# Transformer layer on eight cores: the token buffer is cleared during attention, scatters go tile by tile, x gets five buffers and the first expert weight comes in four parts

## The reference, cut to what matters

```python
xn = _layernorm(x)
s  = _L0_attn_ref(xn, Wq, Wk, Wv, Wo, norm_w)
h  = xn + _mla(_rmsnorm(xn, g1), ...)            # h2 in the kernel
t  = _rmsnorm(h, g2)                             # rows that are routed
top_v, top_i = top_k(t @ gate_w, 2); gates = softmax(top_v)
out = h + sum over the 2 experts of gate * (silu(t @ w1[e]) @ w2[e])
return x + s * _silu(out)
```

## Time and profile before

| | us |
|---|---|
| median of 3 runs (range) | 1723.77 (1721.16 to 1821.45) |
| profiled execution, time | 1732.94 |
| profiled execution, span of its slowest core (core 6) | 1731.4 |
| spans of the 8 cores | 1681.5 to 1731.4 |
| TensorE busy | 1386.5 (80%) |
| VectorE / ScalarE / GpSimd busy | 723.6 / 584.8 / 384.7 |
| attention, from `p2w` issue to last `a_mul` | 475.2 to 873.5 |
| projection and routing, to the first `up` matmul | 873.5 to 1055.25 |

### The profile page before, as it was taken

One profiled execution on the slowest core, in us unless ns is written; L12 is line 12 of the kernel. 1 busy time (PEld: TensorE's weight loads), 2 busy tenths in 40 slices (PEclk: granted clock), 3 DMA queues, 4 the chain that ended last, 5 costly groups with the idle time before them and its releaser, 6 DMA issues.

```text
span 1731.4 us, 24621 instructions; the slowest of 8 cores (1681.5 to 1731.4 us)
## 1 busy us (share of the span) xinstructions
PE 1386.5 (80%) x7665; PEld 613.4 (35%) x7665; DVE 723.6 (42%) x1206; ACT 584.8 (34%) x736; POOL 384.7 (22%) x453
## 2 busy tenths in 40 slices
PE   0768899999967788888647506999999999998457
PEld 0224445544311222222113303555545455554122
DVE  2347766647655555434426630121221212122266
ACT  1112322212245688999603202222222222222121
POOL 4203322247542221211102330000000000005620
PEclk9988999999956899999869857999999999999689
DMA  9744435433197000000076778997999998928698
GB/s 189 152 92 92 98 68 83 77 92 95 47 181 244 1 1 1 1 1 1 0 146 223 204 153 143 189 188 152 200 171 189 206 180 158 202 70 307 198 295 312
DMA packets 148038, 233.73 MB, mean 135 GB/s; under 512 B 74672, under 2 KB 82224, under 8 KB 147888
## 3 DMA queue, kind: packets, MB, share of 16 engines
q0 software_dynamic: 49456, 124.53, 38.3%
q1 hardware_dynamic: 98432, 107.21, 21.7%
HBM read 231.33 MB, written 66.65 MB: 172 GB/s over the span
## 4 chain that ended last, share of the span: by engine, by line
PE 59%; DMA 12%; DVE 12%; issue 8%; ACT 4%; SPq 2%; POOL 2%; DVEq 0%; ACTq 0%; POOLq 0%; PEldq 0%
PE ps L1433 13%; PE pA L1401 7%; PE pB L1401 7%; PE pA L211 4%; PE pA L261 4%; PE ps L790 4%; ACT ap L805 3%; PE pA L754 3%; DMA p4a<-ybuf,rcpos 2%; DMA p4x<-x 2%; PE pB L754 2%; PE pw L790 2%; PE pA L215 2%; DVE ap L825 2%; PE pA L276 2%
## 5 line engine op out<-in xcount | busy, mean ns | idle before, releaser
L1433 PE MATMUL ps<-p3w,mhT 128*128 128x512 bf16 x1152 | 256.2, 381 | 2.7 <-issue 2.7
L805 ACT ACTIVATE ap<-pA,p2nmub 128x1024 bf16<-128x1024 f32 (+1 forms) x160 | 176.5, 1103 | 63.8 <-PE pA L754 58.6
L1556 DVE TENSOR_SCALAR my<-ps,mgate 128x512 f32<-128x512 f32 x78 | 58.3, 750 | 317.1 <-PE ps L1433 316.0
L211 PE MATMUL pA<-fxT,fw 128*128 128x512 bf16 x512 | 130.5, 411 | 69.9 <-DMA fxT<-fxb 42.3
L1433 PEld LDWEIGHTS ps<-p3w,mhT 128*128 128x128 bf16 x1152 | 111.6, 98 | 131.6 <-issue 5.1
L790 PE MATMUL ps<-ap,p2vaug 128*68 128x512 bf16 (+1 forms) x320 | 125.5, 392 | 38.3 <-DVE ap L825 37.2
L1517 ACT ACTIVATE mh<-pA 128x512 bf16<-128x512 f32 x78 | 46.3, 598 | 307.8 <-PE pA L1401 296.2
L805 ACT ACTIVATE ap<-pB,p2nmub 128x1024 bf16<-128x1024 f32 (+3 forms) x160 | 142.4, 890 | 22.6 <-PE pB L754 22.1
L1401 PE MATMUL pA<-p3w,mxT 128*128 128x512 bf16 x576 | 132.7, 384 | 5.5 <-issue 5.5
L1401 PE MATMUL pB<-p3w,mxT 128*128 128x512 bf16 x576 | 130.2, 379 | 1.5 <-issue 1.5
L211 PEld LDWEIGHTS pA<-fxT,fw 128*128 128x128 bf16 x512 | 51.2, 104 | 136.2 <-issue 92.5
(11 more groups left out here) (235 smaller groups left out, 2220.6 us busy)
## 6 DMA issues: line engine op xcount, KB each, us to landing
p3w<-w POOLq DMA_DIRECT2D x16, 4096.0 KB, 40.5
ybuf<-my SPq DMA_DIRECT2D x36, 512.0 KB, 8.4
ybuf<-zero POOLq DMA_DIRECT2D x1, 11776.0 KB, 73.2
mx<-hbuf SPq DMA_DIRECT2D x36, 257.5 KB, 8.0
fx<-x SPq DMA_DIRECT2D x16, 512.0 KB, 5.8
oxn<-x SPq DMA_DIRECT2D x16, 512.0 KB
h_sp<-oh SPq DMA_DIRECT2D x16, 512.0 KB, 3.7
p4hh<-h_sp SPq DMA_DIRECT2D x4, 2048.0 KB, 23.1
```

The lines of the kernel that those rows point to most:

```text
L211: m = t.matmul(bank, wv[:, n // 8, k, 128 * m0:128 * (m0 + 1)], xv[:, k, :], start=(k == 0), stop=(k == DK - 1))
L805: a.activation(dst[:, :, 0:w], src[:, :, 0:w], AF.Exp, bias=c.p2nmub[:, p % 8:p % 8 + 1]).then_inc(c.a_exp, 1)
L1433: m = t.matmul(c.ps(4 + sl), c.mhT[:, 128 * k:128 * (k + 1)], c.p3w2[:, o:o + 512], start=(k == 0), stop=(k == 15))
L1556: v.tensor_scalar_mul(c.my[n % 2][:, sl * 512:(sl + 1) * 512], c.ps(4 + sl), c.mgate[n % 2][:, :]).then_inc(c.m_yev, 1)
```

## The change

1. `hbuf` is cleared whole, all 8 regions of 2176 rows, at the start of the attention: 8 more DMAs from GpSimd behind the one of `ybuf`. The clears in `p3_sync` and their table (`tabzero`) go. GpSimd waits for all 8 clears before the first scatter.
2. x has five buffers; the first five tiles are asked for when the last value matmul of the attention is done (`a_pv`), the others after each store of h2.
3. TensorE waits for the gate weight only ahead of its first use, in turn 3.
4. `oh3b` has 12 rows instead of 8 (`row_ends` with it), `ossq` two.
5. Scatters go tile by tile: two in each turn from i = 8 on.
6. The first expert weight comes in four parts, at i = 2, 5, 8, 11.
7. Slot 0 uses weight buffer 0 without reading tables.

```diff
@@ clear_results, called first in att_gpsimd
+    tokens = c.D["hbuf"].ap().rearrange("(e p r d) -> e p r d", p=128, r=REGION // 128, d=ROW * 2)
+    for e in range(NEXP):
+        g.dma_start(tokens[e], c.zero[:, :].bitcast(U8).unsqueeze(1).broadcast_to(
+            [128, REGION // 128, ROW * 2])).then_inc(c.z_out, 16)
@@ o_sync
-    s.wait_ge(c.a_mul, 2 * NPAIR)
-    for i in range(NTI + 1):
...
+    s.wait_ge(c.a_pv, len(STEPS))
+    for i in range(OXN):
+        load_rest_x(s, c, i)
+    for i in range(NTI):
+        s.wait_ge(c.o_h2, 2 * (i + 1))
+        s.dma_start(tok(c.D["h2_sp"], i), c.oh2[i % 3][:, :]).then_inc(c.o_h2out[i % 3], 16)
+        if i + OXN < NTI:
+            load_rest_x(s, c, i + OXN)
@@ o_tensor
-    t.wait_ge(c.o_gld, 16)
...
+            if j == 0:
+                t.wait_ge(c.o_gld, 16)
@@ o_scalar
-                a.wait_ge(c.o_r3, 2 * i - 1)
                 a.wait_ge(c.o_sq, i)
+            if i >= 2:
+                a.wait_ge(c.o_r3, 2 * (i - 2) + 1)
@@ o_vector
-            if j >= 8:
-                v.wait_ge(c.o_scat[2 * (j % 4)], 16 * (j // 4 - 1))
-                v.wait_ge(c.o_scat[2 * (j % 4) + 1], 16 * (j // 4 - 1))
+            if j >= 12:
+                v.wait_ge(c.o_scat[j - 12], 32)
@@ route_tables
-    v.tensor_tensor(c.rzero[:, :], c.ps(5, 0, 8), c.rcon[:, 32:40], OP.add).then_inc(c.r_zero, 1)
-    v.wait_ge(c.r_zero, 1)
-    v.tensor_scalar_mul(c.tabzero[:, :], c.rzero[:, :], 2.0 * ROW).then_inc(c.r_zero, 1)
@@ o_gpsimd
-    load_w1(g, c, 0)
-    for i in range(NTI + 5):
+    for i in range(NTI + 8):
...
+        if i in (2, 5, 8, 11):
+            load_first_w1(g, c, i // 3)
+        if i == 8:
+            g.wait_ge(c.z_out, 16 * NEXP)
+        if i >= 8:
+            scatter(g, c, hb, i - 8)
+def scatter(g, c, hb, j):
+    g.wait_ge(c.r_pos, 2 * (j // 4 + 1))
+    g.wait_ge(c.o_h3, j + 1)
+    for k in range(2):
+        g.indirect_dma_start(
+            hb, bass.IndirectOffsetOnAxis(c.rpos[:, 16 * k + j:16 * k + j + 1], 0),
+            c.oh3b[:, ROW * (j % 12):ROW * (j % 12 + 1)].bitcast(U8), None
+            ).then_inc(c.o_scat[min(j, 4)], 16)
+def load_first_w1(g, c, q):
+    g.dma_start(c.p3w1[:, 2 * q * EXPD:2 * (q + 1) * EXPD].rearrange("p (k n) -> p k n", n=EXPD),
+                rows3(c.D["w1_0"])[:, 2 * q:2 * (q + 1), :]).then_inc(c.w1ld[0], 16)
@@ p3_sync
-    for e in range(NEXP):
-        with s.register(f"zero{e}") as r:
-            s.reg_load(r, c.tabzero[0:1, e:e + 1])
-            row = s.snap(r, donate=True, min_val=0, max_val=(HROWS - 128) * ROW * 2)
-            s.dma_start(hb[bass.ds(row, 128 * ROW * 2)].rearrange("(p n) -> p n", p=128),
-                        c.zero[:, :].bitcast(U8)).then_inc(c.z_out, 16)
     s.wait_ge(c.r_tab, 19)
...
-    s.wait_ge(c.z_out, 16 * NEXP)
@@ p3_tensor
-    new_w1(0)
-    up(0, 0)
-    up(0, 1)
+    t.wait_ge(c.w1new, 1)
+    t.sem_inc(c.w1new, -1)
+    t.wait_ge(c.m_xev, 1)
+    up_with(0, 0, 0)
+    up_with(0, 1, 0)
@@ regions
+    region(w1_end - DK * EXPD * 2, [("oxn", DM, F32, OXN)])
+    region(route, [("oh2", DM, F32, 3), ("oh3b", 12 * ROW, BF16, 0),
```

More of the change, by code:

```diff
@@ L903, with load_rest_x @@
 RD = 28
-TD = 14
+OXN = 5
 def o_sync(s, c):
-    s.wait_ge(c.a_mul, 2 * NPAIR)
-    for i in range(NTI + 1):
[L910 to L917, removed]
+    s.wait_ge(c.a_pv, len(STEPS))
[6 more added lines that the diff above has]
+            load_rest_x(s, c, i + OXN)
     for q in range(3):
         s.wait_ge(c.o_h2out[q], 16 * len(range(q, NTI, 3)))
+def load_rest_x(s, c, i):
+    s.dma_start(c.oxn[i % OXN][:, :], tok(c.D["x"], i)).then_inc(c.o_xnr[i % OXN], 16)
 def o_tensor(t, c):
@@ L945, in o_tensor @@
                 m = t.transpose(c.pt[:, 128 * k:128 * (k + 1)],
-                                c.oh3b[:, ROW * (j % 8) + 128 * k:ROW * (j % 8) + 128 * (k + 1)], c.ident[:, :])
+                                c.oh3b[:, ROW * (j % 12) + 128 * k:ROW * (j % 12) + 128 * (k + 1)], c.ident[:, :])
             m.then_inc(c.o_tpe, 1)
@@ L976, in o_scalar @@
             if i:
-                a.wait_ge(c.o_r3, 2 * i - 1)
                 a.wait_ge(c.o_sq, i)
+            if i >= 2:
+                a.wait_ge(c.o_r3, 2 * (i - 2) + 1)
             a.activation(c.osqs[:, :], c.oh2[i % 3][:, :], AF.Square,
-                         accum_out=c.ossq[:, :]).then_inc(c.o_sq, 1)
+                         accum_out=c.ossq[i % 2][:, :]).then_inc(c.o_sq, 1)
         j = i - 2
@@ L1013, in o_vector @@
             v.wait_ge(c.o_r3, 2 * (j + 1))
-            if j >= 8:
-                v.wait_ge(c.o_scat[2 * (j % 4)], 16 * (j // 4 - 1))
-                v.wait_ge(c.o_scat[2 * (j % 4) + 1], 16 * (j // 4 - 1))
-            v.scalar_tensor_tensor(c.oh3b[:, ROW * (j % 8):ROW * (j % 8) + DM], c.oh2[j % 3][:, :], c.or3[:, j:j + 1],
+            if j >= 12:
+                v.wait_ge(c.o_scat[j - 12], 32)
+            v.scalar_tensor_tensor(c.oh3b[:, ROW * (j % 12):ROW * (j % 12) + DM], c.oh2[j % 3][:, :], c.or3[:, j:j + 1],
                                    c.g2b[:, :], OP.mult, OP.mult).then_inc(c.o_h3, 1)
@@ L1200, in o_gpsimd @@
                 g.wait_ge(c.o_r3, 2 * i)
-            g.tensor_scalar(c.oms[:, :], c.ossq[:, :], 1.0 / DM, 1e-6, OP.mult,
+            g.tensor_scalar(c.oms[:, :], c.ossq[i % 2][:, :], 1.0 / DM, 1e-6, OP.mult,
                             OP.add).then_inc(c.o_r3, 1)
@@ L1279, in p3_sync @@
     hb = c.D["hbuf"].ap()
-    s.wait_ge(c.z_set, 1)
-    s.wait_ge(c.r_zero, 2)
-    for e in range(NEXP):
-        with s.register(f"zero{e}") as r:
-            s.reg_load(r, c.tabzero[0:1, e:e + 1])
-            row = s.snap(r, donate=True, min_val=0, max_val=(HROWS - 128) * ROW * 2)
-            s.dma_start(hb[bass.ds(row, 128 * ROW * 2)].rearrange("(p n) -> p n", p=128),
-                        c.zero[:, :].bitcast(U8)).then_inc(c.z_out, 16)
     s.wait_ge(c.r_tab, 19)
-    for q in range(8):
-        s.wait_ge(c.o_scat[q], 64)
-    s.wait_ge(c.z_out, 16 * NEXP)
+    for j in range(4):
+        s.wait_ge(c.o_scat[j], 32)
+    s.wait_ge(c.o_scat[4], 32 * 12)
     def load(n):
@@ L1732, in build_program @@
     route = region(w1_end, [
-        ("ogw", DK * NEXP, BF16, 0), ("omh", 1, F32, 0), ("oms", 1, F32, 0), ("ossq", 1, F32, 0),
+        ("ogw", DK * NEXP, BF16, 0), ("omh", 1, F32, 0), ("oms", 1, F32, 0), ("ossq", 1, F32, 2),
         ("or3", NTI, F32, 0), ("rlg", 32, F32, 0), ("rtop", 32, F32, 0), ("ridx", 32, U32, 0),
@@ L1741, in build_program @@
         ("rj", 40, F32, 0), ("rpar", 40, F32, 0), ("rrowf", 40, F32, 0), ("tabrow", 40, I32, 0),
-        ("tabnew", 40, I32, 0), ("tabval", 40, I32, 0), ("tabodd", 40, I32, 0), ("tabzero", 8, I32, 0), ("rzero", 8, F32, 0)])
+        ("tabnew", 40, I32, 0), ("tabval", 40, I32, 0), ("tabodd", 40, I32, 0)])
     c.tablast = c.rcmp[:, 0:40].bitcast(I32)
-    region(route, [("oxn", DM, F32, 2), ("oh2", DM, F32, 3), ("oh3b", 8 * ROW, BF16, 0),
+    region(w1_end - DK * EXPD * 2, [("oxn", DM, F32, OXN)])
+    region(route, [("oh2", DM, F32, 3), ("oh3b", 12 * ROW, BF16, 0),
                    ("oh3T", DM, BF16, 2), ("osqs", DM, BF16, 0)])
```

14 lines of the change are left out of this document (7 added, 7 removed).

## The result

The changed kernel takes 1988.7 us (median of four runs, 1987.0 to 2121.7) against 1727.1 of the kernel before: ratio 1.1525, interval [1.1472, 1.1577]. A run in which the cores of one die show a lower granted clock, as in the one of 2121.7, comes out longer whatever the kernel, and all ratios here leave such runs out, while the medians include them. It is slower by 15%, where 1754 was forecast with a range up to 1780. The profiled span of the slowest core (core 6 again) grows from 1731.4 to 1985.9, by 254.5 us.

What follows compares the result with a forecast made beforehand. It took TensorE to bound most of the span, and transfers and VectorE the 181.8 us between attention and first `up`. An 82 us hold minus 52 gain gave +30 on the 1723.8 median: 1754 us, own range 1734 to 1772, overall 1668 to 1780.

Steps and rivals of the forecast that it cites:

- The list has an end: Start of the attention: GpSimd's DMA list fills, so GpSimd waits inside the issue, with additions, inversion, masks and TensorE behind.
- The eighth goes once the first has landed: Start of the attention: the last `hbuf` clear is issued when the first has landed, at a cost of 82 us.
- the longer hold: Rival at the attention's start: last clear goes after the second lands, 1773 us, or the fourth, 1813; chance 0.18.
- The rate of a clear: Clears of `hbuf` in the attention: 19.7 us each, the middle of 12.8 at 350 GB/s and 26.7 at 168.
- the first rival: No hold at the attention's start: the queue takes all clears at once, net -50 us, 1674; chance 0.27.
- The gain: Sum of the savings, mostly between attention and first expert matmul: 52 us, 43 to 60.
- (a): Start of the projection: TensorE no longer waits for the gate weight before its first matmul, gain 11.6 us.
- (b): The 16 projection tiles: 76.6 us without DMA waits instead of 108.0, 4 charged for transfers, gain 27.4 us.
- third rival: Projection bound by transfers: x tiles, stores, weight parts and scatters share engines; gain 30, time 1776 us; chance 0.07.
- (c): Tail from tile 15's addition to the first slot load: 35.4 us instead of 50.2, gain 14.8 (10 to 19).
- (d): Slot 0 without tables: one or two register loads saved, gain 1 us (0 to 2).
- (e): GpSimd's queue in the projection: scatters and issues delay the power VectorE waits for, -2.5 us (0 to -6).

Runs made afterwards that it cites:

- e1: The changed kernel with the first clear of `hbuf` on a semaphore of its own, the other seven on the shared one; 1779.2 us in a single run.
- e9: The kernel of e4 again, letter for letter, timed in more rounds; 1695.1 us, ratio 0.9795 against the kernel before.
- e4: The changed kernel with the eight clears issued by SyncE, after its transposes and once `ybuf` has landed, none from GpSimd; 1689.1 us in a single run.
- e3: The changed kernel with the clears' zeros in pieces of 2048 bytes laid end to end, the last 0.2 MB not cleared; 1831.2 us in a single run.
- e5: e4 with rows of 2112 bytes instead of 2060 in `hbuf`, `oh3b` and `mx`; 1675.6 us, ratio 0.9679 against the kernel before.
- e10: e5 with TensorE waiting for the gate weight ahead of its first projection matmul again; 1682.2 us, ratio 0.9727 against the kernel before.
- e12: e5 with the first five x tiles asked for after the last scaling instead of the last value matmul; 1678.6 us, ratio 0.9705 against the kernel before.
- e6: e4 with the last two parts of the first expert weight asked for at i = 16 and 18; 1701.5 us, ratio 0.9794 against the kernel before.
- e7: e4 with the four parts of the first expert weight asked for at i = 0, 2, 4, 6; 1699.3 us, ratio 0.9752 against the kernel before.
- e8: e4 with scatters in blocks of four tiles again, the ring of 12 rows kept; four runs from 1691.2 to 1801.9 us, no ratio.
- e11: The changed kernel with rows of 2112 bytes alone, clears still on GpSimd ahead of the additions; 1827.9 us in a single run.

## Why the prediction was wrong

The direction of each half and the outline of the cost were right; the sum was wrong because two links of that mechanism were, and two terms of the gain.

**The list has an end: right.** GpSimd was held in issue, the additions stood behind it, and the inversion, the masks and TensorE behind those. The count fits as well. Behind 560 pieces three clears of 136 went (968), a fourth did not, even with the 64 of `p2w` gone (1040 with it), and it went when the weight's 128 were gone too (912). Then, with `ybuf`'s 368 gone, three more (952 in all, 1088 with the eighth). So the list takes 968 pieces per DMA engine and not 1040, by these rows; and without any room of `p2w` to count on, the eighth clear, held at 952 + 136, says not 1088. The 1024 that I had estimated from the reserve on the Trainium skill's page SBUF — State Buffer (SBUF size) agrees with the trace: it lies between 968 and 1040.

**"The eighth goes once the first has landed": the step that failed.** With a semaphore of its own for the first clear it holds: e1 takes 84 us more than e9 (90 more than e4), close to the 82 of the forecast. That closeness is in part luck. On core 1 the first inversion is 102 later than e4's (600.0 and 498.2), since `ybuf` landed at 557.1 in it and not at the 550.6 of the forecast, and the clear took 32.8 and not 19.7. The attention keeps all of it (495.6 us against 394.2); the time is nearer to 82 because the projection is 6.8 us shorter and what follows 6.7. With the semaphore as the diff has it, the eighth waited for all seven. I had read `.then_inc(c.z_out, 16)` and given it no part in the sum. Of the forecast's candidates (`ybuf`, first, second, fourth clear) the seventh was not one, so even the longer hold, my rival on the slower side, ended at 1813.

**The rate of a clear: 34.2 us, outside the bounds of 12.8 and 26.7.** I took the middle of "12.8 us at 350 GB/s and 26.7 at 168" from windows of other transfers, and had the warning in hand: the slowest window of the profile, 168 GB/s with engines full, was one with clears of 2060-byte rows in it, and `ybuf` with its pieces of 2048 bytes was the one at 350. I gave no reason for the difference. e3 and e5 show what goes with it: 2048 and 2112 bytes go at 345 to 351 GB/s, 2060 at 111 to 151. Together: seven clears of 34.2 us are 239 us behind `ybuf`, and 548.4 + 239.2, then 0.4 to the issue, 1.3 of it and 8.5 of additions lead to the inversion at 797.9, 295.6 later than before. Of the 213 us between that and the forecast's 82, the six further clears at the forecast's 19.7 are 118 and the slower rate of all seven is 101, while the earlier `ybuf` and the shorter additions take 6 back. The additions took 8.5 rather than 12.3 us, since all eight were due at once.

The Trainium skill's advice (DMA: Bandwidth & Descriptors, Rules for kernel authors) to issue a DMA early and wait for it late was one ground of the first rival; the trace contradicts it for this case, since the issue itself was the wait: 301.5 us in three holds. (The page's own reason is narrower than the one I gave: that the fixed setup cost overlaps.) The same page (Specifications) names read-modify-write below 512 bytes as what costs line rate; here pieces four times as long lost more than half of it, and no run shows whether that is the same mechanism.

**The gain: 41.5 instead of 52.** (a) The start came out as written, 11.4 for 11.6, but only in part for the reason given: with x asked for early the load takes 2.8 us, and e10 puts the moved wait alone at 3 to 5 us. Without the early x (e12) the moved wait would have been worth the forecast's 12, but then VectorE waits 5 us for x. (b) Tiles 22.9 for 27.4. The term that failed is "16 scatters of 0.26 MB, 4.2 MB". Each tile is scattered twice, once per expert: 32 scatters and 8.4 MB. In the trace after, the packets of these scatters take 43.5 us of all 16 engines, not 12 to 22. In e5 the same rows take 22.7, so 20.8 are the row size and the rest is the count. With 41 + 28 + 43.5 the stage needs 113 us of DMA, not 86; all its transfers in the trace (the slot loads among them) take 124 of its 140 us on all 16 engines. This is nearest to my third rival, a projection bound by transfers, which I gave 0.07 and priced at a gain of 30. That the projection is bound so is argued from these sums and from e5; e6 and e7 moved transfers and gained nothing, and e12 shows that not every microsecond of transfer counts. (c) Tail 5.0 for 14.8, below its lower bound of 10: the last scatter landed 17.3 after its issue, not 5. (The forecast's own terms add up to 36.0, not 35.4: 1024.06 + 3.7 + 1.2 + 0.5 - 993.49.) With rows of 2112 bytes it lands after 2.9, and from tile 15 to the slot load pass 29.7 us on core 6 and 35.9 on core 1. (d) 2.1 for 1. (e) The -2.5 for GpSimd's queue measured nothing: VectorE shows no wait for it with scatters tile by tile, but 11.3 us in e8's blocks.

With the rate mended (e5), the stage is 128.4 to 128.8 us and the gain 53. That agrees with 52 in sum only, which is luck: the tiles are slower than forecast (82.4 and 87.5 us against 80.6), the tail on core 6 faster.

**What would show it**, in short: the first inversion, put near 584, was at 797.9; one of the last clears, put near 570, came at 788; the first matmul 0.3 us after the last scaling came 0.5 after it; no x wait of over 5 us held (there was none on core 6); tile 15 at 77 to 86 after the first matmul held (85.1); the slot load 31 to 40 after that did not (45.2); 125 to 135 from the last scaling to `up` did not (140.3).

## What to carry to other kernels

Before bulk DMAs are put ahead of work on GpSimd, count their pieces per DMA engine against what its list holds, and look at which semaphores the older ones raise: here the issue was a wait, and the DMAs that shared a semaphore were released as one. Bulk clears belong on a queue behind which nothing is due (here SyncE: 294 us), or between the pieces of work. And take a transfer's rate from a row with the same piece size: a row of 2060 bytes cost a factor of 2.3 or more in clears and 1.9 in scatters (43.5 against 22.7 us) against one of 2112, which moves more bytes.

## What the runs showed of the hardware that I had not expected

- GpSimd held in issue got room back by semaphore. With seven clears on one semaphore the eighth went 0.4 us after the seventh had landed, at 788.0; with the first clear on its own, 0.3 us after the first, at 590.2 (e1).
- Writes of 2060-byte rows: 111 to 154 GB/s with the engines full, issued by GpSimd or by SyncE, with the other engines of the core idle (changed kernel) or busy (e4, 135 to 141 GB/s from 560 to 640). 2048 bytes: 351. 2112 bytes: 345 to 350. In the trace, GpSimd's queue carries two rows in one packet: on average 493 ns for 4120 bytes (changed kernel) and 195 for 4224 (e11); SyncE's has one row in each, 270 ns for 2060 bytes (e9) and 102 for 2112 (e5). Whether it is the length of a piece or where its rows start was not separated: a row length that is no multiple of 64 changes both.
- Reads of the same rows are not slow: in the first slot loads a packet of 2060 bytes takes 109 ns on average (changed kernel, core 6) and one of 2112 bytes 127 (e5, core 6).
- The list of GpSimd held 968 pieces per DMA engine and not 1040 (changed kernel, clears three and four).
- 16 KB of gate weight landed in 2.8 us on idle engines (e10), in 11.2 beside the first weight and x tiles (kernel before), and in 12.1 and 14.1 beside x tiles without the weight (e12).
